# The first spline stage of a four-layer graph network: 125 basis functions by 8 chunk columns in place of 25 by 5 by 8

## The reference, cut to what matters

```python
pos = pseudo * (KS - 1)                     # pseudo: [E, 3] edge coordinates, KS = 5
i0 = jnp.clip(jnp.floor(pos), 0, KS - 2).astype(jnp.int32)
frac = pos - i0
...                                         # basis: products of frac or 1 - frac, 8 corners; idx: their cells of 125
h = jnp.ones((N, 1), x.dtype)
h = jax.nn.elu(spline_conv(h, row, col, basis, idx, stn1_w, stn1_b))    # stn1_w: [125, 1, 64]
```

## Time and profile before

| | us |
|---|---|
| median of 3 runs | 7522.84 |
| lowest, highest | 7507.2, 7532.14 |
| span of the profiled execution (first to last instruction) | 7483.0 |
| TensorE matmul busy | 4661.0 (62%) |
| GpSimd busy | 4710.4 (63%) |
| VectorE busy | 4075.2 (54%) |
| ScalarE busy | 1652.2 (22%) |

### The profile page before, as it was taken

The page is one execution under the profiler, slowest core; times in us unless marked ns, Lnnn a source line. Parts: engine busy times, 40 slices in busy tenths (PEclk is TensorE's granted clock), DMA queues, the critical chain, the costliest instruction groups (busy, mean ns, idle before and its releaser), DMA issues. The chain is left out here.

```text
span 7483.0 us, 94326 instructions
## 1 busy us (share of the span) xinstructions
PE 4661.0 (62%) x31067; PEld 3407.2 (46%) x31067; DVE 4075.2 (54%) x8023; ACT 1652.2 (22%) x2811; POOL 4710.4 (63%) x4319
## 2 busy tenths in 40 slices
PE   5444443866647777777674668999992444444433
PEld 4444442655535555555453434555551333333322
DVE  7555554779945555555551316777763444444433
ACT  1111110128723344443330000000001222222211
POOL 2777776010067777777644247777756777777773
PEclk9999999769978888888887789999996777777766
DMA  4222220023322222222976571111111111111285
GB/s 74 75 77 76 71 77 21 21 47 160 154 59 49 49 49 49 50 49 49 40 37 210 175 247 42 37 37 37 37 34 20 19 18 17 17 17 18 17 15 14
DMA packets 388446, 441.45 MB, mean 59 GB/s; under 512 B 241139, under 2 KB 312320, under 8 KB 387981
## 3 DMA queue, kind: packets, MB, share of 16 engines
q0 software_dynamic: 137696, 130.26, 17.1%
q1 hardware_dynamic: 191113, 286.63, 12.1%
q10 hardware_dynamic: 59568, 23.69, 1.4%
HBM read 358.46 MB, written 82.34 MB: 59 GB/s over the span
## 5 line engine op out<-in xcount | busy, mean ns | idle before, releaser
L951 POOL DMA_INDIRECT at_far<-att_table,at_rec x1184 | 1390.0, 1174 | 806.7 <-DMA at_rec<-rec_r 398.7
L1508 POOL DMA_INDIRECT p_far<-table,p_rec x1184 | 1331.8, 1125 | 459.6 <-issue 360.2
L2140 PE MATMUL g_l_ps_sum<-g_l_row,g_l_of 128*128 128x392 f32 x3224 | 1072.5, 494 | 19.7 <-DVE g_l_of L2092 19.1
L534 POOL DMA_INDIRECT rec_r<-so_r_rec,so_r_place x806 | 835.0, 1036 | 245.5 <-issue 245.5
L2068 POOL DMA_INDIRECT g_l_got<-table,g_l_index x806 | 826.6, 1026 | 245.5 <-issue 245.5
L2140 PEld LDWEIGHTS g_l_ps_sum<-g_l_row,g_l_of 128*128 128x128 f32 x3224 | 609.7, 190 | 483.1 <-DVE g_l_of L2092 47.0
L1406 PE MATMUL p_ps_outer<-p_spread,p_basis 128*25 128x40 f32 (+1 forms) x4736 | 765.4, 343 | 76.2 <-DVE p_spread L1352 70.3
L1406 PEld LDWEIGHTS p_ps_outer<-p_spread,p_basis 128*25 128x25 f32 (+1 forms) x4736 | 652.9, 184 | 195.9 <-issue 95.8
L1406 PE MATMUL at_bank<-p_spread,p_basis 64*125 64x256 f32 x4736 | 636.9, 426 | 42.3 <-ACT p_outer L1461 42.3
L489 PE MATMUL so_r_look<-so_r_table,so_r_lo_t 128*128 128x26 f32 x1612 | 425.1, 434 | 310.8 <-DVE so_r_table L433 310.8
L1432 PE MATMUL p_ps_by_chunk<-p_fold,p_run 128*128 128x32 f32 x148 | 37.8, 395 | 924.2 <-DVE p_run L1362 924.2
(11 more groups left out here) (457 smaller groups left out, 6159.2 us busy)
## 6 DMA issues: line engine op xcount, KB each, us to landing
adjacent<-ad_by_chunk SPq DMA_DIRECT2D x74, 800.0 KB, 3.3
so_r_row<-pad_src SPq DMA_DIRECT2D x62, 832.0 KB, 6.1
g_l_counts<-adjacent SPq DMA_DIRECT2D x60, 800.0 KB, 7.3
g_l1d_counts<-adjacent SPq DMA_DIRECT2D x59, 800.0 KB, 7.0
so_r_low<-pad_lo_src SPq DMA_DIRECT2D x62, 416.0 KB, 4.6
at_far<-att_table,at_rec POOLq DMA_INDIRECT x1184
p_far<-table,p_rec POOLq DMA_INDIRECT x1184, 2.5
rec_r<-so_r_rec,so_r_place POOLq DMA_INDIRECT x806, 2.1
```

The costliest lines, as they stand in the source:

```text
L534: pool.indirect_dma_start(out=o.rec[:, :], out_offset=bass.IndirectOffsetOnAxis(ap=place[b][:, j:j + 1], axis=0), in_=rec[b][:, j, :], in_ ...
L951: pool.indirect_dma_start(out=far[b][:, t, :], out_offset=None, in_=g.att_table[:, :], in_offset=bass.IndirectOffsetOnAxis(ap=rec[b][:, t, ...
L1508: pool.indirect_dma_start(out=sl.far[b][:, t, :], out_offset=None, in_=table[:, :], in_offset=bass.IndirectOffsetOnAxis(ap=sl.rec[b][:, t, ...
L2140: last = nc.tensor.matmul(ps_sum[k][:], of4[b][:, j, :, :].rearrange("p k f -> p (k f)"), row1[b][:, j, k * COLS:(k + 1) * COLS], start=Fa ...
```

## The change

The stage is written anew, without the class `Spline`; nothing else changes but the call, which gives the weights as 125 × 64.

- ScalarE makes the hats, in eight activations a block, each over 96 elements a partition, straight from the records: relu(1 − 4x), 4x, relu(4x − 1), relu(4x − 2), relu(4x − 3) into `hat`, and the falling sides relu(2 − 4x), relu(3 − 4x), 4 − 4x into `down`.
- VectorE takes the minimum of the three inner hats, makes `there` (1 where the slot has an edge), spreads it into 8 columns (128 × 256), makes the 25 pairs and from these all 125 bases (two operations of 2000 elements a partition each).
- TensorE's outer products have the 125 bases as the stationary operand and the 8 columns as the moving one, into one bank of 125 × 256. One product with the weights a block follows, then the scan and transposes as before.
- Nearly all tiles are double, and the stages of a block are set further apart: TensorE does outer products of n, transposes of n − 2, weights of n − 1; VectorE makes block n and scans n − 2; ScalarE makes hats of n + 1, copies n, stores n − 2. `keep` is loaded by SyncE into two tiles, a block ahead. The scan takes its start from the last column of the other `run` tile, so the copy of the carry goes.
- The first four blocks and the last are written out, the others run in a loop of two.

```diff
-def stage_spline_ones(nc, g, name, weights, fin, fout, sums, scattered):
+def stage_spline_ones(nc, g, name, weights, sums, scattered):
...
+    C8, V, K, OUT = o.per_tile, o.vb, 125, 64
...
+        def all_blocks(eng, one, restart=None):
+            for n in range(lead):
+                one(n, n % 2, n // 2)
+            with eng.Fori(lead // 2, lead // 2 + loops) as i:
...
+                for b in two:
+                    one(i * 2 + b, b, i)
...
             @block.sync
...
+                def one(n, b, turn):
+                    if early(n) >= 2:
+                        sp.wait_ge(spreads, n - 1)
+                    sp.dma_start(rec[b][:], rec_v[:, bass.ds(n * TB, TB), :]).then_inc(rec_in[b], 16)
+                    if early(n) >= 3:
+                        sp.wait_ge(scanned, n - 2)
+                    if early(n) >= 1:
+                        load_keep(n - 1, 1 - b)
...
+            @block.scalar
...
+                def make_hats(n, b, turn):
+                    act.wait_ge(rec_in[b], turn * 16 + 16)
+                    if early(n) >= 2:
+                        act.wait_ge(spreads, n - 1)
+                    at = rec[b][:, :, 1:4].bitcast(F32)
+                    up, to = (lambda k: hat[b][:, :, :, k]), (lambda k: down[b][:, :, :, k])
+                    nc.scalar.activation(up(0), at, ACT.Relu, bias=offs[:, 0:1], scale=-4.0)
+                    nc.scalar.mul(up(1), at, 4.0)
+                    for k in (2, 3, 4):
+                        nc.scalar.activation(up(k), at, ACT.Relu, bias=offs[:, k:k + 1], scale=4.0)
+                    nc.scalar.activation(to(0), at, ACT.Relu, bias=offs2[:, 0:1], scale=-4.0)
+                    nc.scalar.activation(to(1), at, ACT.Relu, bias=offs2[:, 1:2], scale=-4.0)
+                    nc.scalar.activation(to(2), at, ACT.Identity, bias=offs2[:, 2:3], scale=-4.0).then_inc(hats, 1)
+                def copy_products(n, b):
+                    act.wait_ge(products, n + 1)
+                    if early(n) >= 2:
+                        act.wait_ge(made, n - 1)
+                    nc.scalar.copy(outer[b][:], ps_outer[b][:]).then_inc(outers, 1)
...
+                def one(n, b, turn):
+                    if early(n) < last_block:
+                        make_hats(n + 1, 1 - b, turn + b)
+                    copy_products(n, b)
+                    if early(n) >= 2:
+                        store_rows(n - 2)
...
             @block.vector
...
+                def one(n, b, turn):
+                    dve.wait_ge(hats, n + 1)
+                    ch.put(nc.vector.tensor_scalar(there[:], rec[b][:, :, 0], float(N), None, ALU.is_lt))
+                    ch.step(nc.vector.tensor_tensor(hat[b][:, :, :, 1:4], hat[b][:, :, :, 1:4], down[b][:], ALU.min))
+                    if early(n) >= 2:
+                        dve.wait_ge(products, n - 1)
+                    ch.put(nc.vector.tensor_mul(spread[b][:], there[:].unsqueeze(2).to_broadcast([P, TB, C8]), o.mask[:].unsqueeze(1).to_broadcast([P, TB, C8])))
...
+                        ch.put(nc.vector.tensor_mul(pair[:, ts, :].rearrange("p t (a b) -> p t a b", a=5),
+                                                    h(0, ts).unsqueeze(3).to_broadcast(b55), h(1, ts).unsqueeze(2).to_broadcast(b55)))
+                    ch.wait()
...
+                        last = nc.vector.tensor_mul(basis[b][:, ts, :].rearrange("p t (a b) -> p t a b", b=5),
+                                                    pair[:, ts, :].unsqueeze(3).to_broadcast(b255), h(2, ts).unsqueeze(2).to_broadcast(b255))
+                    last.then_inc(spreads, 1)
+                    if early(n) >= 2:
+                        scan(n - 2, b, turn - 1)
...
             @block.tensor
...
+                def outer_products(n, b):
+                    pe.wait_ge(spreads, n + 1)
+                    if early(n) >= 2:
+                        pe.wait_ge(outers, n - 1)
+                    for t in range(TB):
+                        last = nc.tensor.matmul(ps_outer[b][:, t * C8:(t + 1) * C8], basis[b][:, t, :], spread[b][:, t, :], start=True, stop=True)
+                    last.then_inc(products, 1)
...
+                def through_weights(n, b):
+                    pe.wait_ge(outers, n + 1)
+                    if early(n) >= 1:
+                        pe.wait_ge(scanned, n)
+                    nc.tensor.matmul(ps_out[:], w[:], outer[b][:], start=True, stop=True).then_inc(made, 1)
+                def one(n, b, turn):
+                    outer_products(n, b)
+                    if early(n) >= 2:
+                        turn_rows(n - 2, b)
+                    if early(n) >= 1:
+                        through_weights(n - 1, 1 - b)
```

More of the change, by code:

```diff
@@ L1570, in _ @@
                 sl.end_scalar(act)
-def stage_spline_ones(nc, g, name, weights, fin, fout, sums, scattered):
-    with ExitStack() as c:
[L1579 to L1583, removed]
+def stage_spline_ones(nc, g, name, weights, sums, scattered):
+    o = g.R
+    C8, V, K, OUT = o.per_tile, o.vb, 125, 64
+    parts, two = V // P, range(2)
+    half = TB // 2
+    with ExitStack() as c:
+        sb = lambda nm, shape, dt=F32: c.enter_context(nc.sbuf_tensor(f"{name}_{nm}", shape, dt))
+        ps = lambda nm, shape: c.enter_context(nc.psum_tensor(f"{name}_{nm}", shape, F32))
+        sem = lambda nm: new_sem(nc, c, f"{name}_{nm}")
+        w = sb("w", [K, OUT])
+        rec = [sb(f"rec{b}", [P, TB, o.words], I32) for b in two]
+        keep = [sb(f"keep{b}", [OUT, V]) for b in two]
+        hat = [sb(f"hat{b}", [P, TB, 3, 5]) for b in two]
+        down = [sb(f"down{b}", [P, TB, 3, 3]) for b in two]
+        offs, offs2 = sb("offs", [P, 5]), sb("offs2", [P, 3])
+        there, pair = sb("there", [P, TB]), sb("pair", [P, TB, 25])
+        basis = [sb(f"basis{b}", [P, TB, K]) for b in two]
+        spread = [sb(f"spread{b}", [P, TB, C8]) for b in two]
+        outer = [sb(f"outer{b}", [K, V]) for b in two]
+        run = [sb(f"run{b}", [OUT, V]) for b in two]
+        rows = sb("rows", [P, parts, OUT])
+        ps_outer = [ps(f"ps_outer{b}", [K, V]) for b in two]
+        ps_out, ps_rows = ps("ps_out", [OUT, V]), ps("ps_rows", [P, parts, OUT])
+        rec_in, keep_in = [sem(f"rec_in{b}") for b in two], [sem(f"keep_in{b}") for b in two]
+        w_in, near_made, steps, offsets, hats, spreads, scanned = (
+            sem(n) for n in ("w_in", "near_made", "steps", "offsets", "hats", "spreads", "scanned"))
+        products, outers, made, turned, copied, out, seen = (
+            sem(n) for n in ("products", "outers", "made", "turned", "copied", "out", "seen"))
+        rec_v, keep_v = o.rec.rearrange("(p t) w -> p t w", p=P), o.keep.rearrange("(a v) -> a v", a=1)
+        last_block, lead = o.blocks - 1, 4
+        loops = (o.blocks - lead) // 2
+        tail = range(lead + 2 * loops, o.blocks)
+        def all_blocks(eng, one, restart=None):
+            for n in range(lead):
+                one(n, n % 2, n // 2)
+            with eng.Fori(lead // 2, lead // 2 + loops) as i:
+                if restart is not None:
+                    restart()
+                for b in two:
+                    one(i * 2 + b, b, i)
+            if restart is not None:
+                restart()
+            for n in tail:
+                one(n, n % 2, n // 2)
+        early = lambda n: n if isinstance(n, int) else lead
@@ L1591, in _, with load_keep @@
             def _(sp):
[L1592 to L1605, removed]
+                def load_keep(n, b):
+                    sp.dma_start(keep[b][:], keep_v[:, bass.ds(n * V, V)].to_broadcast([OUT, V])).then_inc(keep_in[b], 16)
@@ new lines, in one @@
+                def one(n, b, turn):
[6 more added lines that the diff above has]
+                        load_keep(n - 1, 1 - b)
+                sp.dma_start(w[:], weights).then_inc(w_in, 16)
+                all_blocks(sp, one)
@@ new lines, in _, with store_rows @@
+                sp.wait_ge(scanned, last_block - 1)
+                load_keep(last_block, last_block % 2)
+            @block.scalar
+            def _(act):
+                def make_hats(n, b, turn):
[16 more added lines that the diff above has]
+                    nc.scalar.copy(outer[b][:], ps_outer[b][:]).then_inc(outers, 1)
+                def store_rows(n):
+                    act.wait_ge(turned, n + 1)
+                    if early(n) >= 1:
+                        act.wait_ge(out, n * 16)
+                    nc.scalar.copy(rows[:], ps_rows[:]).then_inc(copied, 1)
+                    act.wait_ge(copied, n + 1)
+                    act.dma_start(sums[bass.ds(n * V, V), :].rearrange("(q p) w -> p q w", p=P), rows[:]).then_inc(out, 16)
+                def one(n, b, turn):
[4 more added lines that the diff above has]
+                        store_rows(n - 2)
+                act.wait_ge(offsets, 1)
+                make_hats(0, 0, 0)
+                all_blocks(act, one)
+                store_rows(last_block - 1)
+                store_rows(last_block)
```

(38 more changed lines are left out.)

13 lines of the change are left out of this document (11 added, 2 removed).

## The result

The changed kernel takes 7731.43 us (7720.61 to 7733.52, 4 runs), the kernel before 7515.24 (7507.2 to 7532.14, 4 runs): a ratio of 1.028, 95% interval 1.0261 to 1.0298, slower by 216 us; forecast were 7727 us. The profiled span grew by 235.4 us, from 7483.0 to 7718.4. Of these 209 us lie in the changed stage; the rest is spread over three later stages with unchanged code, 8 to 9 us in each. A timed run of the changed kernel lasts 2.2 us longer than its span (7720.61 and 7718.4). Taking the same 2.2 us, the traced execution of the kernel before took some 7485 us, an estimate, 22 us less than its fastest timed run.

The account below looks back on a forecast made before the run. TensorE's instruction stream was taken as the bound: blocks going from 9.31 to 14.7 us put the last outer products +205.7 us later, with −2.0 behind them, so 7522.84 + 204 = 7727 us; 80% range 7575 to 7770.

Parts of the forecast that it names:

- The block: Changed stage on TensorE, low clock: outer products 13.4, weights 0.86, transposes 0.3, seams 0.15, together 14.7 us a block.
- the seams: TensorE between its groups of instructions in a block: 0.15 us added, besides some 0.3 us for transposes with their seam.
- the start: Before the stage's first outer product: 2.3 us of hats and 6.9 on VectorE, so 1284.5 us, 2.6 later than before.
- The 39.8 us: Whole kernel: the runs' median stands 39.8 us above the profiled span, taken as launch and end around it.
- The level: TensorE's clock in the changed stage: low throughout, chance 0.74, 7727 us, own range 7700 to 7745.
- three stretches of kindred products: Elsewhere in the trace: 6-column products, twenty of 33 columns, the histogram's 26-column products; all end or stay at the low level.
- What I said the trace would show: Changed stage: loads 320 to 335 ns, granted clock 0.50, blocks 14.7 us apart, VectorE idle about 7 us a block.
- VectorE's whole block: VectorE in the changed stage: 7.35 us a block, 7.6 with step waits, hidden beside TensorE's 14.7 us.
- Serial load and stream: Rival in TensorE's outer products: load and stream not overlapped, 15.5 us a block, 7757 us, chance 0.06.
- The high level: Rival on TensorE's clock: high throughout, 8.2 us a block, 7485 us, faster by 0.5%, chance 0.10.
- the loop through ScalarE: Copy, hats, VectorE, then outer products two blocks on: 8.0 to 8.4 us a block, the bound only at high level.
- The rival's −38 us: High level throughout: −40 us over 36 blocks, +2.6 start, +2.5 last outer products, −3 behind them; chance 0.10.

Follow-up runs that it names:

- e1: Changed kernel with only the first 96 of the 125 bases as stationary columns, the rest left out of the sum: 7617.87 us, ratio 1.012 to the kernel before.
- e3: Changed kernel with 128 moving columns a product instead of 8, the extra ones useless: 7491.59 us, ratio 0.9969 to the kernel before.
- e5: e3 with ScalarE making the hats two blocks ahead instead of one: 8811.5 us on a second chip, ratio 0.9923 to the kernel before.
- e9: e7 with ScalarE making the hats two blocks ahead: 8773.57 us on a third chip, ratio 0.9833 to the kernel before.
- e4: Changed kernel with bases and spread mask in bf16, one instruction a product instead of two: 7435.58 us, ratio 0.9882 to the kernel before.
- e2: Changed kernel with 40 moving columns a product instead of 8: 7734.65 us, ratio 1.0282 to the kernel before.
- e8: Changed kernel with 64 moving columns a product instead of 8: 9068.87 us on a second chip, ratio 1.0212 to the kernel before.
- e7: Changed kernel's order of work with the old product (25 bases, five weight products): 8747.72 us on a second chip, ratio 0.9847 to the kernel before.
- e12: e9 with the 25 bases and the spread third hats in bf16: 8822.9 us on a third chip, ratio 0.9881 to the kernel before.

## Why the prediction was right

*The bound and the direction.* Right: TensorE's stream of instructions was the bound before and after. 13.4 us were forecast for 64 outer instructions, 13.6 measured. e1 shows the price in proportion to the stationary columns.

*The block.* 14.7 us forecast, 14.93 measured. Some 0.1 to 0.2 us are in the outer products (13.53 us from their start to the transposes', 13.6 with the last one's tail, for 13.4) and 0.1 in the seams: weights and transposes with what stands between them take 15.0 − 13.6 = 1.4 us, for 1.3. Times 36 that is 8 us; the start, 1.2 us early, gives some back, and the stage has +209 for +204.

*The number.* 7727 us for 7731.43 is closer than the sum was, partly by luck: the growth was 216 us for 204, and the kernel before came out at 7515.24 instead of 7522.84. The step from span to time was read wrongly. The 39.8 us are not launch and end, which are 2.2 us in the changed kernel's traced run; most of them are how fast the traced execution of the kernel before was. So the span, forecast at 7687 us, was 7718.4. The mechanism does not hang on this.

*The level.* Right, and it decided: the low level throughout. I had argued from three stretches of kindred products. e3 shows it as a cause: same loads, the same 64 instructions, sixteen times the moving columns, and the loads take 189 ns. The Trainium skill, "TensorE: Matmul & The Clock Gate", "Part 1: The HAM clock gate", ties the full clock to sustained activity; the changed stage, busy 551.68 of 552 us at the low level, is not what a reader of that sentence would expect, and the profile's busy time is no measure of it. The level is not the whole of the loss, though. At the high level 64 outer instructions still take 7.25 us (e3, e5), where the old product's take 2.48 in e9, and with the hats two blocks ahead the new product's stage has 340.1 us (e5) and the old one's 270.4 (e9). Against the old product in the new order, the new one loses at either level.

*What I said the trace would show.* Loads of 320 to 335 ns: 331. No wait for the copy or the marks: none. VectorE idle 7 us a block: (236.9 + 59.5)/37 = 8.0. A granted clock of 0.50: wrong, it reads 1.00, though I had noted for the kernel before that the column can't be trusted ahead of its first recorded change. A later stage that changes by more than a few us was to be a sign of being wrong, and three did, by 8 to 9 us each; e3's trace has the same growth there without the longer stage, so it does not speak against the mechanism.

*VectorE and ScalarE.* Basis 4.48 us: 4.39. Eight hats 2.3 us: 2.2, from 1274.48 to 1276.66. No table load before them. VectorE's whole block was forecast at 7.6 us, and e4, where it is the bound, has 7.0. The first product starts at 1283.3 (1284.5 forecast), and behind the last one 5.5 us are left (5.7).

*The rivals.* Serial load and stream: refuted by e2 and e8. The high level: its block of 8.2 us was sized for this kernel with nothing added; at that level e3 has 8.8, and by e5 it is the loop through ScalarE that makes them, as forecast, with 0.6 us more than I had counted; that these lie in its handovers is not shown. The rival's −38 us were −19 there, as 36 blocks of 0.6 us more take back some 20.

*What I had wrong in the rest.* For e7 I took the levels as mixed as before, and so had 8.3 us a block, for 5.8 behind the first blocks; and 3.7 us for the outer products at the high level, where e9 has 2.48. I did not see that the pauses and the level are one matter: the 1 us wait for ScalarE, which I had priced at 1 us a block, cost 2.7 more by the level (98/36).

## What to carry to other kernels

A product with many stationary and few moving columns costs its load, and nothing that the moving side saves comes back; count the stationary columns first. Take TensorE's clock level into the sum before any trade of instructions, read it from the durations of like instructions rather than from busy time, and try the cheap trial: let each product stream more columns than it needs. A short wait on TensorE, repeated in every block, can cost several times its length, so removing it is worth trying alone before the work itself is made anew.

## What the runs showed of the hardware that was not expected

Useless work made a kernel faster: 128 moving columns for 8 took the stage from 594.2 to 365.7 us. One pause of 1.0 us a block took it from 284.2 to 418.3. Halving the outer instructions with bf16 (e12) made the remaining fp32 products take 4.52 us for 2.37. What rule ties the level to the work of a stretch was not settled by these runs, nor why the old product in the new order starts with a stall (45.1 us for e7's first three blocks, 31.0 before).
